# Values and sums of two chunks in one slot, two buffers of exponentials, and two small LayerNorm steps on ScalarE

## The chip, the cores and the metric

The kernel runs on one core of one Trainium2 chip. The metric is the device time of the whole program in microseconds, as the median of several executions. Times inside an execution come from one execution recorded by the hardware profiler.

## What is computed

A cross-attention layer with LayerNorm in fp32: x has 16 batches of 512 rows of 512, the context 16 batches of 77 rows of 512; there are 16 heads of 32.

```
Q = x Wq + bq;  K = ctx Wk + bk;  V = ctx Wv + bv        (16 heads of 32)
attn = softmax(Q K^T / sqrt(32)) over the 77 context rows
out  = (attn V) Wo + bo
result = (out + x - mean) * rsqrt(var + 1e-5) * gamma + beta
```

## The kernel before

The big projections run as three matmuls in TensorE's faster fp32r format: each operand is split into a high part (a ScalarE copy or activation) and a low part (the difference, on GpSimd or VectorE), and high x high, high x low and low x high are summed (xh and xl, qh and ql, ch and cl). `project_context` makes K and part of V first; `attend` does the rest and takes most of the time.

`attend` is a software pipeline of 64 *chunks* g. A chunk is one batch's group of four heads (128 of the 512 columns), so four chunks make a batch, and as many tiles of 128 output rows follow from it. Every engine runs its own `slot(g)` function once per g, in the order written there, through `run`: two rounds of 8 slots and the last ones are written out, the rest is a hardware loop of 8 slots. A slot works on several chunks at different stages; `g.back(n)` is the chunk n slots earlier. Slot g does:

- TensorE: `project_q(g)` into the one bank p_q; `values` and `sums` of chunk g-4 (p_v holds the four heads' values, p_den the sums of the exponentials, from `part` and the selection matrix `sel`); `scores` of g-3 into p_s (two banks, four matmuls a chunk: two after the sums, one each after the second and third step of the output projection); `project_out` of tile g-8 into the one bank p_o, in four steps kc = 0 to 3, one for each chunk of its batch; after each step `rowmax_scores` of g into p_a (two banks, four tiles a chunk).
- ScalarE: `q_high(g)`, the four `exp` of g-3 into `prob`, with `square` of tile g-9 after the second; `load_residual`; `ctx_high` of g-4 (cx to ch), `normalize` of tile g-10, `split_x_high` of x tile g+5 (xt to xh), then the load of a further x tile.
- VectorE: `sum_keys` of g-4 (prob to part), `minus_mean_over_std` of tile g-10 (nmr), `add_residual` of tile g-9 (frees p_o), `q_low`, `invert_sums` (rec, then its transposed spread rden) and `divide` (p_v by rden into cx) of g-4, `variance_of_squares` of g-9 (ve), four `row_maxima` of g, and `turn_maxima` in odd slots.
- GpSimd: `scale` and `shift` of tile g-11, `add_bo` of g-8, `ctx_low` of g-4 (cx - ch to cl), `inverse_std` of g-9 (rstd), `split_x_low` of x tile g+5 (xt - xh to xl).
- SyncE issues the loads of K, V, the q splits rearranged by head (z) and the row maxima, and the stores of finished tiles after `shift`.

There is one `prob`, one `part`, one `rec`, one p_v bank. `project_out` of a batch's first tile (t = 0) waits at kc = 0 for ch and cl of all four chunks (lines 647 to 649):

```
if t == 0:
    pe.wait_ge(ch_ready, m.over(QT, 1, KC))
    pe.wait_ge(cl_ready, m.over(QT, 1, KC))
```

`m.over(QT, 1, KC)` counts the chunks up to the end of tile m's batch. The first tile of batch b is projected in slot 4b + 8; the batch's last chunk, 4b + 3, has its values in slot 4b + 7. Two of the p banks serve at the end for other things (gamma_tail and beta_tail, the last tiles' p_o).

Of the kernel before, what the change touches and what calls it, by code (L numbers as in the profile page):

```python
# [26 lines left out]
P = 128  # L27
D = 512
# [75 lines left out]
def project_context(nc, a, keep, kh_dram, kl_dram, v_dram, B, S2):  # L104
# [12 lines left out]
    with ExitStack() as ctx:  # L117
# [33 lines left out]
        with nc.Block() as block:  # L151
# [172 lines left out]
def attend(nc, a, keep, kh_dram, kl_dram, v_dram, out, B, S, S2):  # L324
# [21 lines left out]
    with ExitStack() as ctx:  # L346
# [6 lines left out]
        def sem(name):  # L353
# [20 lines left out]
        ysum, ssd, nmean = (sb(n, [P, 4, 1], F32) for n in ("ysum", "ssd", "nmean"))  # L374
        p_q, p_v, p_den, p_o = (psum(n) for n in ("p_q", "p_v", "p_den", "p_o"))
# [25 lines left out]
        mv_ready, ve_ready, nmr_ready, const_dve, y_last_scaled, y_last_done, nmean_ready, rows_tail = (  # L401
            sem(n) for n in ("mv_ready", "ve_ready", "nmr_ready", "const_dve", "y_last_scaled", "y_last_done", "nmean_ready", "rows_tail"))
# [12 lines left out]
        gamma_tail, beta_tail = p_s[1], p_den  # L415
# [160 lines left out]
        def _(pe):  # L576
# [14 lines left out]
            def rowmax_scores(g, t):  # L591
# [27 lines left out]
            def values(g):  # L619
# [4 lines left out]
                at_least(pe, cx_ready, g.over(1))  # L624
                for j in range(HC):
                    h = HC * (g.k % NCH) + j
                    nc.tensor.matmul(p_v[DK * j:DK * (j + 1), :], vb[0:S2, g.k // NCH % 2, DK * h:DK * (h + 1)],  # L627
                                     prob[0:S2, j, :], start=True, stop=True)

            def sums(g):  # L630
# [3 lines left out]
                for j in range(HC):  # L634
                    last = nc.tensor.matmul(p_den[DK * j:DK * (j + 1), 0:QB], sel[:], part[:, QB * j:QB * (j + 1)],  # L635
# [44 lines left out]
            def slot(g):  # L680
# [6 lines left out]
                if v.valid(NG) and g.valid(NG):  # L687
                    values(v)
                    sums(v)
# [3 lines left out]
                if not g.valid(NG):  # L693
                    values(v)
# [18 lines left out]
        def _(act):  # L713
            def exp(g, j):
                act.wait_ge(s_summed, g.over(1, 0, HC) + j + 1)
                if j == 0:
                    if g.is_first():
                        act.wait_ge(const_pool, 2)
                    at_least(act, pv_summed, g.over(1))
                    at_least(act, part_ready, g.over(1))  # L720
                nc.scalar.activation(prob[0:S2, j, :], p_s[j % 2][0:S2, :], ACT.Exp, scale=SCALE).then_inc(prob_ready, 1)  # L721
# [26 lines left out]
            def square(m):  # L748
# [4 lines left out]
                                     accum_out=ssd[:, i, :]).then_inc(squared, 1)  # L753

# [113 lines left out]
        def _(dve):  # L868
# [15 lines left out]
            def sum_keys(g):  # L884

                dve.wait_ge(prob_ready, g.over(1, 1, HC))
                at_least(dve, pv_summed, g.over(1))
                nc.vector.tensor_reduce(part[:], prob[0:KP, :, :].rearrange("p h (i r) -> p (h i) r", r=DK),  # L888
                                        AX_X, ALU.add, apply_transpose=True).then_inc(part_ready, 1)

            def invert_sums(g):

                dve.wait_ge(pv_summed, g.over(1, 1))
                at_least(dve, rden_ready, g.over(1))
                nc.vector.reciprocal(rec[:], p_den[:, 0:QB]).then_inc(rec_ready, 1)
                dve.wait_ge(rec_ready, g.over(1, 1))
                at_least(dve, cx_ready, g.over(1))
                nc.vector.transpose(rden[:].rearrange("p (i r) -> p i r", r=DK),  # L898
                                    rec[:].unsqueeze(2).broadcast_to([P, QB, DK])).then_inc(rden_ready, 1)
# [13 lines left out]
            def divide(g):  # L913
# [4 lines left out]
                nc.vector.tensor_tensor(cx[:, i, :], p_v[:], rden[:], ALU.mult).then_inc(cx_ready, 1)  # L918
# [33 lines left out]
            def slot(g):  # L952
# [3 lines left out]
                if v.valid(NG):  # L956
                    sum_keys(v)
                if g.back(LAG_NORMALIZE).valid(NS):
# [5 lines left out]
                if v.valid(NG):  # L964
                    invert_sums(v)
                    divide(v)
                if m.valid(NS):
# [45 lines left out]
            invert_sums(Slot(0, NG - 1))  # L1013
            divide(Slot(0, NG - 1))
# [24 lines left out]
        def _(pool):  # L1039
# [4 lines left out]
            nc.gpsimd.memset(prob[DK * 2:KP, :, :], 0.0).then_inc(const_pool, 1)  # L1044
# [148 lines left out]
```

## Time and profile before

| | us |
|---|---|
| median of 3 runs (lowest to highest) | 623.35 (622.33 to 623.76) |
| profiled execution, its own time | 622.21 |
| its span, first to last instruction | 620.4 |
| TensorE matmuls busy | 594.8 (96%) |
| VectorE busy | 496.9 (80%) |
| ScalarE busy | 362.9 (58%) |
| GpSimd busy | 443.7 (72%) |

The profile's records name an instruction by its line, its engine, its operation, and out<-in by the names of the tiles. PE is TensorE, PEld its weight loads, DVE VectorE, ACT ScalarE, POOL GpSimd. A matmul's record is longer than the step to the next one, because matmuls overlap; the difference of two starts is what one costs. The fp32 matmuls of values and sums appear as two records each.

### The profile page before, as it was taken

How to read it: one execution, taken by the hardware profiler on the slowest of the kernel's cores; microseconds unless marked ns; L12 is line 12 of the kernel's file. 1: busy time of each engine (PE TensorE's matmuls, PEld its weight loads, DVE VectorE, ACT ScalarE, POOL GpSimd, SP SyncE). 2: the span in 40 equal slices, each digit the busy share in tenths (PEclk: the TensorE clock that was granted, in tenths of full speed). 3: DMA queues.
4: the chain of work that ended last, by engine and by line, in shares of the span. 5: the costliest groups of instructions: out<-in, count | busy, mean ns of one | idle time of the engine just before them, and what ended most of it. 6: DMA issues, size and time to landing. Idle time of an engine off the chain costs nothing.

```text
span 620.4 us, 12034 instructions
## 1 busy us (share of the span) xinstructions
PE 594.8 (96%) x3336; PEld 430.5 (69%) x3336; DVE 496.9 (80%) x913; ACT 362.9 (58%) x674; POOL 443.7 (72%) x395
## 2 busy tenths in 40 slices
PE   5998999999999999999999999999999999999992
PEld 5986765677777777777777777777777777777562
DVE  5423468888888888888888888888888888898776
ACT  5621235566666666666666666666666666655562
POOL 1335024648888888888888888888888888888785
PEclk9999999999999999999999999999999999999997
DMA  8859878988979898989898987979897989796523
GB/s 306 308 224 185 205 181 224 206 189 193 235 192 232 212 215 214 224 203 219 201 229 205 221 226 193 235 201 227 207 219 205 211 218 231 196 221 168 168 76 128
DMA packets 93392, 129.58 MB, mean 209 GB/s; under 512 B 49936, under 2 KB 49936, under 8 KB 93360
## 3 DMA queue, kind: packets, MB, share of 16 engines
q1 hardware_dynamic: 74352, 94.42, 60.8%
q10 hardware_dynamic: 19008, 34.78, 21.8%
q8 instruction: 15, 0.25, 0.2%
q14 instruction: 17, 0.14, 0.1%
HBM read 53.94 MB, written 24.35 MB: 126 GB/s over the span
## 4 chain that ended last, share of the span: by engine, by line
PE 87%; DVE 3%; issue 1%; ACT 1%; DVEq 0%; ACTq 0%
PE p_q L586 29%; PE p_o L652 27%; PE p_s L616 10%; PE p_v L627 10%; PE p_a L602 6%; PE p_o L99 3%; DVE nm L933 1%; PE p_a L669 1%; PE p_den L635 1%; DVE rden L898 0%; PE p_q L669 0%; ACT prob L721 0%; DVE part L888 0%; PE p_s L669 0%; ACT qh L736 0%
## 5 line engine op out<-in xcount | busy, mean ns | idle before, releaser
L721 ACT ACTIVATE prob<-p_s 77x512 f32<-77x512 f32 x256 | 143.2, 591 | 103.3 <-PE p_s L616 93.0
L1069 POOL TENSOR_TENSOR cl<-cxt,ch 128x512 fp32r<-128x512 f32 x64 | 83.1, 1299 | 110.0 <-ACT ch L746 110.0
L933 DVE TENSOR_REDUCE nm<-p_a 128x4 f32<-128x308 f32 x256 | 115.9, 475 | 49.1 <-PE p_a L602 48.0
L888 DVE TRANSPOSE_TENSOR_REDUCE part<-prob 96x64 f32<-96x2048 f32 x64 | 146.4, 2287 | 1.6 <-issue 1.3
L736 ACT ACTIVATE qh<-p_q,bq_col 128x512 fp32r<-128x512 f32 x64 | 44.0, 687 | 124.6 <-PE p_q L586 124.6
L586 PE MATMUL p_q<-xh,wqh 128*128 128x512 f32 x256 | 101.1, 395 | 1.7 <-PEq L151 1.7
L586 PE MATMUL p_q<-xl,wqh 128*128 128x512 f32 x256 | 101.2, 395 | 0.0
L586 PE MATMUL p_q<-xh,wql 128*128 128x512 f32 x256 | 101.0, 394 | 0.0
L616 PE MATMUL p_s<-z,ks 97*77 97x512 f32 x256 | 95.6, 413 | 2.4 <-ACT prob L721 2.4
L652 PE MATMUL p_o<-woh,ch 128*128 128x512 f32 x240 | 95.4, 398 | 0.8 <-issue 0.7
L652 PE MATMUL p_o<-wol,ch 128*128 128x512 f32 x240 | 94.6, 394 | 0.0
L652 PE MATMUL p_o<-woh,cl 128*128 128x512 f32 x240 | 94.3, 393 | 0.0
L1050 POOL TENSOR_TENSOR xl<-xt,xh 128x512 fp32r<-128x512 f32 x60 | 77.2, 1287 | 20.0 <-ACT xh L728 20.0
L602 PE MATMUL p_a<-kb,qh 128*128 128x308 f32 x256 | 79.0, 311 | 2.9 <-DVE nm L933 2.8
L1064 POOL TENSOR_TENSOR y<-y,beta_row 128x512 f32<-128x512 f32 x58 | 75.3, 1299 | 4.5
L1076 POOL TENSOR_TENSOR xn<-xn,bo_row 128x512 f32<-128x512 f32 x60 | 77.5, 1291 | 0.0
L1060 POOL TENSOR_TENSOR y<-y,gamma_row 128x512 f32<-128x512 f32 x58 | 74.5, 1285 | 0.0
L627 PE MATMUL p_v<-prob,vb 77*32 77x512 f32 x512 | 68.2, 605 | 0.0
L602 PEld LDWEIGHTS p_a<-kb,qh 128*128 128x128 f32 x256 | 48.3, 189 | 22.9 <-DVE nm L933 7.7
L925 DVE SCALAR_TENSOR_TENSOR ql<-p_q,bq_col,qh 128x512 fp32r<-128x512 f32 x64 | 47.9, 748 | 17.0 <-ACT qh L736 13.5
L652 PEld LDWEIGHTS p_o<-woh,ch 128*128 128x128 f32 x240 | 45.3, 189 | 17.3 <-issue 3.8
L586 PEld LDWEIGHTS p_q<-xh,wqh 128*128 128x128 f32 x256 | 48.0, 188 | 13.3 <-issue 2.1
(128 smaller groups left out, 930.1 us busy)
## 6 DMA issues: line engine op xcount, KB each, us to landing
z<-qh SPq DMA_DIRECT2D x256, 128.0 KB, 3.8
z<-ql SPq DMA_DIRECT2D x124, 128.0 KB, 4.8
xn<-in_x ACTq DMA_DIRECT2D x60, 256.0 KB, 3.3
out_dram<-y SPq DMA_DIRECT2D x60, 256.0 KB, 4.3
xt<-in_x_t ACTq DMA_DIRECT2D x58, 256.0 KB, 5.0
ks<-k_high SPq DMA_DIRECT2D x32, 154.0 KB, 4.8
cx<-in_ctx_t SPq DMA_DIRECT2D x4, 616.0 KB, 6.0
k_high<-kth SPq DMA_DIRECT2D x4, 616.0 KB, 3.6
```

What stands on the lines that cost most here:

```text
L586: last = nc.tensor.matmul(p_q[:], w[:, kc, P * c:P * (c + 1)], x[:, i, kc, :], start=(kc == 0 and n == 0), stop=(kc == KC - 1 and n == 2))
L602: nc.tensor.matmul(p_a[t % 2][:, 0:HC * S2], qh[:, g.k // 2 % 2, g.k % 2, P * t:P * (t + 1)], kb[g.k // NCH % 2][:, g.k % NCH, :], start=T ...
L616: nc.tensor.matmul(p_s[j % 2][0:S2, :], ks[0:KR, g.k // NCH % 2, h, :], z[0:KR, i, j, g.k % 2, :], start=True, stop=True).then_inc(s_summe ...
L627: nc.tensor.matmul(p_v[DK * j:DK * (j + 1), :], vb[0:S2, g.k // NCH % 2, DK * h:DK * (h + 1)], prob[0:S2, j, :], start=True, stop=True)
L652: last = nc.tensor.matmul(p_o[:], x[:, i, kc, P * t:P * (t + 1)], w[:, kc, :], start=(kc == 0 and n == 0), stop=(kc == KC - 1 and n == 2))
L721: nc.scalar.activation(prob[0:S2, j, :], p_s[j % 2][0:S2, :], ACT.Exp, scale=SCALE).then_inc(prob_ready, 1)
L888: nc.vector.tensor_reduce(part[:], prob[0:KP, :, :].rearrange("p h (i r) -> p (h i) r", r=DK), AX_X, ALU.add, apply_transpose=True).then_i ...
L933: nc.vector.tensor_reduce(nm[:, t, g.k % 2:HALF:2], p_a[t % 2][:, 0:HC * S2].rearrange("p (h k) -> p h k", k=S2), AX_X, ALU.max, negate=Tr ...
L1050: nc.gpsimd.tensor_tensor(xl[:, i, n.k % KC, :], xt[:, n.k % 2, :], xh[:, i, n.k % KC, :].bitcast(F32), ALU.subtract).then_inc(xl_ready, 1)
L1064: nc.gpsimd.tensor_tensor(rows(m), rows(m), beta[:], ALU.add).then_inc(y_done, 1)
L1069: nc.gpsimd.tensor_tensor(cl[:, i, g.k % NCH, :], cx[:, g.k % 2, :], ch[:, i, g.k % NCH, :].bitcast(F32), ALU.subtract).then_inc(cl_ready, 1)
L1076: nc.gpsimd.tensor_tensor(xn[:, m.k % 2, :], xn[:, m.k % 2, :], bo[:], ALU.add).then_inc(xb_ready, 1)
```

## The change

TensorE's `values` and `sums` of two chunks now come together in odd slots (`values_of_pair`): p_v has two banks, and one set of four matmuls sums both chunks into 32 columns of p_a's first bank, behind the 308 that the row maxima use. The odd slot's first `rowmax_scores` therefore waits for the reciprocal of those sums, which is one for both chunks; the sums wait for the maxima that read that bank. `prob`, `part` and `rec` have two buffers. The last four chunks (`single`) go one by one as before, with p_v[1] for their sums.

With w = g-5, the chunk before g-4: VectorE does `spread` (the transposition, now by itself) and `divide` of the even chunk in the odd slot (w there) and of the odd chunk at the start of the next even slot (w there); its `sum_keys` of the even chunk stands after the second row maximum of the even slot. ScalarE's `ctx_high` follows: at the end of an odd slot for the even chunk, first in the even slot for the odd one. GpSimd does both `ctx_low` in the even slot: of e = g-6 first, and of w after `scale` and `shift`. `project_out` waits for ch and cl of one chunk at each kc instead of all four at kc = 0.

In slots of the loop the variance moves from VectorE to ScalarE (`variance`, after `square`), and so does the mean over the deviation (`mean_over_std`, two operations, ahead of `normalize`); in the tail VectorE does them as before. The scratch memory for GpSimd-issued DMAs is set to 2048.

```diff
+        den_pair = p_a[0][:, HC * S2:HC * S2 + 2 * QB]
+        den_single = p_v[1][:, 0:QB]
...
 def rowmax_scores(g, t):
+                if t == 0 and g.k % 2 == 1 and g.back(LAG_PV).valid(NG):
+                    pe.wait_ge(rec_ready, g.back(LAG_PV).over(1, 1))
...
+            def values_of_pair(g):
+                at_least(pe, cx_ready, g.over(1, -1))
+                values(g.back(1))
+                values(g)
+                pe.wait_ge(part_ready, g.over(1, 1))
+                at_least(pe, rec_ready, g.over(1, -1))
+                at_least(pe, max_ready, g.over(1, LAG_PV, QT) - 1)
+                for j in range(HC):
+                    last = nc.tensor.matmul(den_pair[DK * j:DK * (j + 1), :].rearrange("p (i r) -> p i r", r=QB), sel[:],
+                                            part[:, :, QB * j:QB * (j + 1)], start=True, stop=True)
+                last.then_inc(pv_summed, 2)
...
 def project_out(m, kc):
-                    if t == 0:
-                        pe.wait_ge(ch_ready, m.over(QT, 1, KC))
-                        pe.wait_ge(cl_ready, m.over(QT, 1, KC))
                     at_least(pe, y_ready, m.over(1))
+                if t == 0:
+                    pe.wait_ge(ch_ready, m.over(QT, 0, KC) + kc + 1)
+                    pe.wait_ge(cl_ready, m.over(QT, 0, KC) + kc + 1)
...
 # TensorE's slot
-                if v.valid(NG) and g.valid(NG):
-                    values(v)
-                    sums(v)
+                if v.valid(NG) and g.valid(NG) and g.k % 2 == 1:
+                    values_of_pair(v)
...
 def exp(g, j):
-                    at_least(act, pv_summed, g.over(1))
-                    at_least(act, part_ready, g.over(1))
+                    at_least(act, pv_summed, pair_end(g.back(2)))
+                    at_least(act, part_ready, g.over(1, -1))
...
+            def variance(m):
+                i = m.k % 4
+                act.wait_ge(squared, m.over(1, 1))
+                nc.scalar.activation(ve[:, i, :], ssd[:, i, :], ACT.Identity, bias=keep["eps"][:],
+                                     scale=1.0 / D ** 3).then_inc(ve_ready, 1)
+            def mean_over_std(m):
+                i = m.k % 4
+                act.wait_ge(rstd_ready, m.over(1, 1))
+                nc.scalar.mul(over_d[:, i, :], rstd[:, i, :], -1.0 / D).then_inc(over_d_ready, 1)
+                act.wait_ge(over_d_ready, m.over(1, 1))
+                nc.scalar.activation(nmr[:, i, :], ysum[:, i, :], ACT.Copy, scale=over_d[:, i, :]).then_inc(nmr_ready, 1)
...
 # ScalarE's slot
+                w = v.back(1)
+                if g.k % 2 == 0 and w.valid(NG) and not single(w):
+                    ctx_high(w)
                 if g.valid(NG):
                     q_high(g)
...
                     square(m)
+                    if g.valid(NG):
+                        variance(m)
...
                     exp(s, 3)
-                if v.valid(NG):
+                if g.k % 2 == 1 and w.valid(NG) and not single(w):
+                    ctx_high(w)
+                if v.valid(NG) and single(v):
                     ctx_high(v)
+                if g.back(LAG_NORMALIZE).valid(NS) and g.valid(NG):
+                    mean_over_std(g.back(LAG_NORMALIZE))
...
 # VectorE's slot
+                w = v.back(1)
+                if g.k % 2 == 0 and w.valid(NG) and not single(w):
+                    spread(w)
+                    divide(w)
-                if v.valid(NG):
+                if v.valid(NG) and (g.k % 2 == 1 or not g.valid(NG)):
                     sum_keys(v)
...
+                if v.valid(NG) and not single(v) and g.k % 2 == 1:
+                    invert_sums(v)
+                    spread(w)
+                    divide(w)
...
                         row_maxima(g, t)
+                        if t == 1 and v.valid(NG) and g.k % 2 == 0:
+                            sum_keys(v)
...
 # GpSimd's slot
+                w, e = v.back(1), v.back(2)
+                if g.k % 2 == 0 and e.valid(NG) and not single(e):
+                    ctx_low(e)
                 if g.back(LAG_SCALE).valid(NS):
                     scale(g.back(LAG_SCALE))
                     shift(g.back(LAG_SCALE))
+                if g.k % 2 == 0 and w.valid(NG) and not single(w):
+                    ctx_low(w)
                 if b.valid(NS):
                     add_bo(b)
-                if v.valid(NG):
+                if v.valid(NG) and single(v):
                     ctx_low(v)
```

## Rows read from the trace of the kernel before

**Rows 1.** The page's chain that ended last, by line, shares of the span.
```profile
PE p_q L586 29%; PE p_o L652 27%; PE p_s L616 10%; PE p_v L627 10%; PE p_a L602 6%; PE p_o L99 3%; DVE nm L933 1%; PE p_a L669 1%; PE p_den L635 1%; DVE rden L898 0%; PE p_q L669 0%; ACT prob L721 0%; DVE part L888 0%; PE p_s L669 0%; ACT qh L736 0%
```

**Rows 2.** Busy us (instructions) in 295 to 345 us: PE, PEld, DVE, ACT, POOL, clock, DMA.
```profile
295.00:345.00 50.00, 50.00 (x291) 35.98 (x290) 43.85 (x83) 32.38 (x62) 41.36 (x37) 1.00 0.87 211
```

**Rows 3.** Timeline of TensorE, slot 31: start us, length us, engine, line, operation.
```profile
302.30 0.39 PE L586 MATMUL p_q<-xh,wqh 128*128 128x512 f32 x1
...
304.85 0.39 PE L586 MATMUL p_q<-xh,wql 128*128 128x512 f32 x1
305.18 1.06 PE L627 MATMUL p_v<-prob,vb 77*32 77x512 f32 x8
306.06 0.23 PE L635 MATMUL p_den<-part,sel 96*32 96x16 f32 x8
306.22 0.69 PE L616 MATMUL p_s<-z,ks 97*77 97x512 f32 x2
...
309.38 0.39 PE L616 MATMUL p_s<-z,ks 97*77 97x512 f32 x1
...
309.75 0.40 PE L652 MATMUL p_o<-woh,ch 128*128 128x512 f32 x1
...
310.45 0.30 PE L602 MATMUL p_a<-kb,qh 128*128 128x308 f32 x1
310.59 0.39 PE L586 MATMUL p_q<-xh,wqh 128*128 128x512 f32 x1
```

**Rows 4.** Wait list: who waited for whom: us in total, times, longest us.
```profile
POOL cl L1069 <- ACT ch L746: 110.0, 62, 8.0
```

**Rows 5.** Timeline of ScalarE, border of slots 31 and 32; idle time before in brackets.
```profile
309.14 1.25 ACT L721 ACTIVATE prob<-p_s 77x512 f32<-77x512 f32 x2 [0.65 <-PE p_s L616]
...
310.30 0.61 ACT L746 CAST ch<-cxt 128x512 fp32r<-128x512 f32 x1
...
311.52 0.62 ACT L728 CAST xh<-xt 128x512 fp32r<-128x512 f32 x1
```

**Rows 6.** Timeline of GpSimd, from the border of slots 31 and 32.
```profile
310.99 1.30 POOL L1069 TENSOR_TENSOR cl<-cxt,ch 128x512 fp32r<-128x512 f32 x1 [1.35 <-ACT ch L746]
...
312.76 1.29 POOL L1050 TENSOR_TENSOR xl<-xt,xh 128x512 fp32r<-128x512 f32 x1
314.00 1.29 POOL L1060 TENSOR_TENSOR y<-y,gamma_row 128x512 f32<-128x512 f32 x1
315.38 1.30 POOL L1064 TENSOR_TENSOR y<-y,beta_row 128x512 f32<-128x512 f32 x1
316.63 1.30 POOL L1076 TENSOR_TENSOR xn<-xn,bo_row 128x512 f32<-128x512 f32 x1
```

**Rows 7.** Timeline of VectorE, slots 31 and 32.
```profile
306.95 0.71 DVE L898 STREAM_TRANSPOSE rden<-rec 128x512 f32<-128x512 f32 x1
...
310.79 0.48 DVE L933 TENSOR_REDUCE nm<-p_a 128x4 f32<-128x308 f32 x1 [0.36 <-PE p_a L602]
311.30 0.31 DVE L950 STREAM_TRANSPOSE nmt<-nm 128x128 f32<-128x128 f32 x1
311.93 2.31 DVE L888 TRANSPOSE_TENSOR_REDUCE part<-prob 96x64 f32<-96x2048 f32 x1 [0.32 <-issue]
...
314.25 0.68 DVE L880 SCALAR_TENSOR_TENSOR y<-p_o,xn 128x512 f32<-128x512 f32 x1
...
314.86 0.74 DVE L925 SCALAR_TENSOR_TENSOR ql<-p_q,bq_col,qh 128x512 fp32r<-128x512 f32 x1
315.52 0.24 DVE L895 RECIPROCAL rec<-p_den 128x16 f32<-128x16 f32 x1
```

**Rows 8.** Groups by line and shape: busy us, mean ns of one | idle us before, releasers.
```profile
L910 DVE TENSOR_SCALAR nmr<-ysum,rstd 128x1 f32<-128x1 f32 x59 | 10.0, 169 | 0.1
...
L210 ACT ACTIVATE kth<-pk,bk_col 128x360 fp32r<-128x360 f32 x8 | 4.3, 561 | 2.2 <-PE pk L301 2.2
...
L210 ACT ACTIVATE kth<-pk,bk_col 128x512 fp32r<-128x512 f32 x4 | 2.8, 688 | 7.4 <-PE pk L301 5.1 <-DMA k_low<-ktl 2.3
```

More of the change, by code:

```diff
@@ L373, in attend @@
         ve, rstd, nmr = (sb(n, [P, 4, 1], F32) for n in ("ve", "rstd", "nmr"))
-        ysum, ssd, nmean = (sb(n, [P, 4, 1], F32) for n in ("ysum", "ssd", "nmean"))
-        p_q, p_v, p_den, p_o = (psum(n) for n in ("p_q", "p_v", "p_den", "p_o"))
+        ysum, ssd, nmean, over_d = (sb(n, [P, 4, 1], F32) for n in ("ysum", "ssd", "nmean", "over_d"))
+        p_q, p_o = (psum(n) for n in ("p_q", "p_o"))
+        p_v = [psum(f"p_v{i}") for i in range(2)]
         p_s = [psum(f"p_s{i}") for i in range(2)]
@@ L412, in attend @@
                       (p_s[0], prob_ready, NG * HC)]
-        gamma_tail, beta_tail = p_s[1], p_den
+        gamma_tail, beta_tail = p_s[1], p_v[1]
         x_last = [xt[:, 0, :], xt[:, 1, :], bv_row[:], vb[:, B % 2, :]]
@@ L434, in last_tile, with single, pair_end @@
             return None
+        den_pair = p_a[0][:, HC * S2:HC * S2 + 2 * QB]
+        den_single = p_v[1][:, 0:QB]
+        def single(v):
+            return isinstance(v.u, int) and PAIR * v.u + v.k >= NG - LAG_PV
+        def pair_end(v):
+            return v.over(1, 1) if single(v) else Slot(v.u, v.k | 1).over(1, 1)
         def is_last(c):
@@ L623, in values @@
                     pe.wait_ge(vb_in[g.k // NCH % 2], g.over(PAIR, 1, 16))
-                at_least(pe, cx_ready, g.over(1))
+                bank = p_v[0] if single(g) else p_v[g.k % 2]
                 for j in range(HC):
                     h = HC * (g.k % NCH) + j
-                    nc.tensor.matmul(p_v[DK * j:DK * (j + 1), :], vb[0:S2, g.k // NCH % 2, DK * h:DK * (h + 1)],
-                                     prob[0:S2, j, :], start=True, stop=True)
+                    nc.tensor.matmul(bank[DK * j:DK * (j + 1), :], vb[0:S2, g.k // NCH % 2, DK * h:DK * (h + 1)],
+                                     prob[0:S2, g.k % 2, j, :], start=True, stop=True)
+            def values_of_pair(g):
[9 more added lines that the diff above has]
+                last.then_inc(pv_summed, 2)
             def sums(g):
@@ L634, in sums @@
                 for j in range(HC):
-                    last = nc.tensor.matmul(p_den[DK * j:DK * (j + 1), 0:QB], sel[:], part[:, QB * j:QB * (j + 1)],
+                    last = nc.tensor.matmul(den_single[DK * j:DK * (j + 1), :], sel[:], part[:, g.k % 2, QB * j:QB * (j + 1)],
                                             start=True, stop=True)
@@ L893, in invert_sums, with spread @@
                 dve.wait_ge(pv_summed, g.over(1, 1))
[L894 to L896 removed]
+                at_least(dve, rden_ready, g.over(1, 0 if single(g) else -1))
+                if single(g):
+                    nc.vector.reciprocal(rec[:, g.k % 2, :], den_single).then_inc(rec_ready, 1)
+                else:
+                    nc.vector.reciprocal(rec[:], den_pair.rearrange("p (i r) -> p i r", r=QB)).then_inc(rec_ready, 2)
+            def spread(g):
+                dve.wait_ge(rec_ready, pair_end(g))
                 at_least(dve, cx_ready, g.over(1))
                 nc.vector.transpose(rden[:].rearrange("p (i r) -> p i r", r=DK),
[L899 removed]
+                                    rec[:, g.k % 2, :].unsqueeze(2).broadcast_to([P, QB, DK])).then_inc(rden_ready, 1)
             def variance_of_squares(m):
                 i = m.k % 4
+                if PAIR * m.u + m.k == NG - LAG_NORM:
+                    dve.wait_ge(rstd_ready, NG - LAG_NORM)
                 dve.wait_ge(squared, m.over(1, 1))
@@ L955, in slot @@
                     add_residual(m)
-                if v.valid(NG):
+                w = v.back(1)
[3 more added lines that the diff above has]
+                if v.valid(NG) and (g.k % 2 == 1 or not g.valid(NG)):
                     sum_keys(v)
-                if g.back(LAG_NORMALIZE).valid(NS):
+                if g.back(LAG_NORMALIZE).valid(NS) and not g.valid(NG):
                     minus_mean_over_std(g.back(LAG_NORMALIZE))
@@ L1013, in _ @@
             invert_sums(Slot(0, NG - 1))
+            spread(Slot(0, NG - 1))
             divide(Slot(0, NG - 1))
```

36 lines of the change are left out of this document (21 added, 15 removed).

## The prediction

> **What bounds the kernel now.** I read the page's chain of waits first: over 80% of it are TensorE's lines, the projections p_q (29%) and p_o (27%), then p_s and p_v at 10% each [rows 1]. The busy times by stretch say the same of the middle: TensorE busy for all of 50 us at a granted clock of 1.00 [rows 2]. So while the pipeline is full, one slot's time is the time of its matmuls, and whatever shortens TensorE's list shortens the kernel, as long as nothing new makes it wait. I therefore read the timelines of TensorE, ScalarE, GpSimd and VectorE around the border between slot 31 (from 302.30) and slot 32 (from 310.59) [rows 3, 5 to 7], since 32 is a slot in which a new batch's output projection begins (k a multiple of 4). The other engines have spare time: the wait list shows GpSimd waiting 110 us for ch over 62 waits [rows 4], some 1.7 us a slot. Spare time is an average, though; what the change has to pass is the order inside one slot.
>
> **TensorE's own list.** In slot 31 the last p_q starts at 304.85 and the first p_s at 306.22, 1.37 us later, where neighbouring matmuls of 512 columns are 0.23 apart (eleven steps from 302.30 to 304.85) [rows 3]. In an even slot the values and sums go away: minus 1.37 - 0.23 = 1.14 us. The odd slot gets a second set of values: p_v at 305.18 to p_den at 306.06 is 0.88 us a set [rows 3]; its weights load while the set before streams. The joint sums have 32 columns for 16. The old step from p_den to p_s is 0.16 us, so the extra is between nothing and another 0.16; I take 0.01, since 16 more columns are little beside 512. A pair of slots gets 1.14 - 0.88 - 0.01 = 0.25 us shorter, bounds 0.10 (sums twice as long) and 0.32 (the p_s pair, which runs 0.06 behind its step after the sums, recovers too). There are 28 pairs in slots 8 to 63: minus 7.0 us, bounds 2.8 and 9.0.
>
> **VectorE.** Half of the reciprocals, the variance and the mean leave it in the loop (0.24 us for a reciprocal [rows 7], 0.17 for the mean [rows 8]); it is not on the chain, so this earns nothing by itself. What matters is that spread and divide of the odd chunk now open the even slot, ahead of add_residual, and that the values no longer stand between p_q and p_o there. Counted from the last p_a of an odd slot (310.45): the maximum starts at 310.79 and its turn at 311.30 [rows 7]; spread would start at about 311.6 and take 0.71, divide start at 312.35, add_residual at 313.0 and be ready 0.69 later, at 313.7, 3.2 after p_a (these operations follow each other in some 0.61 to 0.66, as y, ql and rec do from 314.25 to 315.52 [rows 7]). TensorE needs p_o's bank after 0.14 + 12 x 0.23 + 2 x 0.23, 3.4. The copy to ch and q_high behind divide give qh after 3.85, against a first p_a at 4.1. Both pass with 0.2 us to spare: cost nothing, bound 0.3 a pair. In the odd slot, p_a's first bank now waits for the joint reciprocal. Counted from the start of the even slot, 7.1 us long: its second p_a at 5.05, 0.34 later the maximum (0.4), then sum_keys 2.3, two maxima 0.8, sum_keys 2.3, add_residual 0.61, ql 0.66 and rec 0.24, together 12.7, or 5.6 us into the odd slot; TensorE gets to its p_a there after 6.05 (12 p_q, 1.8 of values, 0.2 of sums, two p_s, three p_o). Behind p_a on TensorE stands the whole rest of the slot, so each of these margins would be paid in full if missed.
>
> **The new order on ScalarE and GpSimd, and the wait it makes.** Chunk 4b+3 is the last of its batch. Its spread and divide now happen in slot 4b+8, the slot in which project_out of that batch's first tile begins. The change lets project_out wait for the chunks one at a time, so only its fourth step (kc = 3) needs cl of 4b+3. But on GpSimd this ctx_low is fourth in its slot, behind ctx_low of 4b+2, scale and shift, and the last thing of GpSimd's slot before is split_x_low, which waits for ScalarE's split_x_high, in turn the last thing of ScalarE's slot, behind the fourth exp. That exp waits for the fourth p_s, late in TensorE's slot. So the chain runs from TensorE to TensorE:
> - p_s of slot 31 starts at 309.38 [rows 3]; the second exp of the 1.25 us pair starts at 309.80, ch at 310.30, xh at 311.52 and it ends at 312.14 [rows 5].
> - New ahead of xh are two one-column ScalarE operations, each waiting for the one before on its own engine. No such operation stands in the trace: the same activation takes 561 ns on 360 columns and 688 on 512 [rows 8], a straight line that leaves about 0.26 us for none. Two of them with some 0.05 for each wait: 0.6 us. Lower bound 0.3 (VectorE's price for two small ones), upper 0.95. xh ends at 312.74.
> - GpSimd then does the split 1.24 (312.76 to 314.00), ctx_low 1.25, scale 1.38 (314.00 to 315.38), shift 1.25 (315.38 to 316.63) and ctx_low of 4b+3, 1.30 in full [rows 6]: 6.42 us, so cl is there at about 319.25. The chunk itself is no obstacle: its ch would be ready some 3.1 us into the slot, at 313.7.
> - TensorE gets to kc = 3 at 309.75 - 302.30 = 7.45 us into an old slot [rows 3], and 1.14 earlier in an even one: 310.59 + 6.31 = 316.90.
>
> TensorE stands still for 2.35 us with everything else of the slot queued behind it. It can't be won back: from there to the next fourth p_s of an odd slot three slots later TensorE has no slack, and the chain starts anew from that p_s. In slots with k = 2 mod 4 the same cl comes as late, but nothing asks for it yet. The wait needs a split in the slot before (the last is in slot 58) and a scale and shift in its own (from slot 11 on): slots 12, 16, ... 56, so 12 times. 12 x 2.35 = plus 28.2 us; bounds 12 x 1.9 and 12 x 2.9 (the two small operations, and 0.2 for GpSimd's rows, which are rough).
>
> The Trainium skill ("ScalarE: Activation LUTs", Rules for kernel authors) gives simple multiplies and adds to VectorE, not ScalarE. The rows agree: the mean is one operation of 0.17 us there [rows 8] and two of about 0.26 here. By that rule, with the mean left on VectorE, the wait would be 0.6 shorter and the sum below 7 us lower, still a loss.
>
> **The rest.** Variance sits on ScalarE between square and the third exp; that exp waited for p_s in slot 31 (0.65 us idle in its row, the DMA issue included [rows 5]), and by these spacings it still starts no later than the fourth p_s allows: nothing, bound 0.2 a slot. SP's store waits for shift, now some 7.4 us into the even slot; behind it stand the z loads of the next slot, which wait for ql, some 5 us into that slot, so it costs nothing. No DMA is added and GpSimd issues none, so the smaller scratch costs nothing. The second buffer of exponentials frees exp from the sums of the chunk before, which only the tail can use. Before slot 8 the stages are filling and TensorE is not full; two pairs there and fewer VectorE operations: minus 1.5, bounds 0 and 3. After slot 63, spread and divide of chunk 59 (1.4 us) come ahead of sum_keys, partly repaid by the freed exp: plus 0.5, bounds -1 and +1.5.
>
> **Sum.** The profiled execution took 622.2 us (span 620.4). 622.2 - 7.0 + 28.2 - 1.5 + 0.5 = 642.4. That execution lies 1.1 under the median of 623.35, so on the median's footing 643.5.
>
> **Rivals.**
> - *The wait is hidden (faster).* If GpSimd reaches ctx_low of 4b+3 before 6.3 us of the slot, only TensorE's shorter list is left: 622.2 - 7.0 - 1.5 + 0.5 = 614.2, or 615.3 on the median. For it: GpSimd is idle 1.7 us a slot on average [rows 4], and the waits per chunk were split just here. Against it: the idle time lies ahead of the split, waiting for xh, so it can't be used. It decides at 2.35 us of error in a chain whose members are all rows but 0.6 us. A half-sized wait (1.2 us) would give 628.6, or 629.7; the gain is eaten up from 0.67 us of wait on (8.0 / 12).
> - *Further waits in every pair (slower still).* If the 0.2 us margins at p_o's bank, qh or the reciprocal are missed by 0.3, 28 x 0.3 = 8.4: 652. For it: three margins under half a microsecond with nothing behind them. Against: the stalled slot gives VectorE 2.35 us every fourth slot.
> - *The change does nothing at all* (TensorE reloads and drains between the two value sets for about 0.25, and the wait is hidden): 623.
>
> **How the numbers follow.** The wait as computed 0.77, further waits 0.11, hidden or nearly so 0.10, nothing 0.02. Measured times of this kernel tell differences of 0.2% (1.2 us) from none, so slower is 0.77 + 0.11 = 0.88, same 0.02, faster 0.10. The computed case reaches from 635 to 651 with its bounds; taking in the half-sized wait and part of the further waits I give 630 to 655, and leave 615 outside.
>
> **What would show it.** In the profile after: TensorE's weight load for p_o waiting for GpSimd's cl, about 12 times and some 2.4 us each, 28 us in the wait list; GpSimd's xl waiting for ScalarE's xh in odd slots; even slots of about 7.1 us and 9.5 us in turn, odd ones of 9.15; nm, rec and y hardly waited for by TensorE. A wait list without cl under p_o proves the main step wrong and leaves the rival of 615; waits of p_o for y or p_a for rec and qh show the second rival. If xh ends less than 0.3 or over 0.95 later than before against its p_s, only the size of the wait was wrong.

## The result: 656.9 us, 5.4% slower, and the profile after

The changed kernel takes 656.86 us (median of 5, 656.57 to 660.08) beside 623.6 of the kernel before in the same rounds: a ratio of 1.0543, 95% interval 1.0526 to 1.0561. The forecast was 643.5, within 630 to 655: the direction held, the size did not. The profiled execution is the longest of the five, 660.08 (span 658.0, mean granted clock 0.970); the other four have 656.6 to 657.0 at about 0.975.

The wait that the prediction computed is there. The page's chain of waits by engine, before and then after, now has GpSimd first, where TensorE stood:

```profile
PE 87%; DVE 3%; issue 1%; ACT 1%; DVEq 0%; ACTq 0%
...
POOL 40%; PE 25%; issue 21%; DVE 4%; ACT 1%; POOLq 0%; DVEq 0%; ACTq 0%
```

The wait list after (total us, times, longest) names the place: p_o's matmul waits for cl exactly 12 times. Its weight load waits there too, put down to "issue" (12 of that row's 17 times). The waits that would have shown the second rival are small:

```profile
POOL xl L1125 <- ACT xh L756: 114.5, 34, 10.4
...
PEld p_o L680 <- issue: 34.0, 17, 2.6
...
PE p_o L680 <- POOL cl L1144: 25.1, 12, 2.3
...
PEld p_o L680 <- DVE y L933: 2.4, 11, 0.8
PE p_a L617 <- DVE nm L996: 2.2, 5, 0.5
```

TensorE at the border of slots 31 and 32, to lay beside [rows 3] (start, length, engine, line, operation, idle time before):

```profile
316.08 0.40 PE L599 MATMUL p_q<-xh,wqh 128*128 128x512 f32 x1
...
324.02 0.39 PE L631 MATMUL p_s<-z,ks 97*77 97x512 f32 x1
...
325.24 0.39 PE L599 MATMUL p_q<-xh,wqh 128*128 128x512 f32 x1
...
329.01 0.47 PE L680 MATMUL p_o<-woh,ch 128*128 128x512 f32 x1 [0.34 <-ACT ch L774]
...
333.98 0.47 PE L680 MATMUL p_o<-woh,ch 128*128 128x512 f32 x1 [1.75 <-POOL cl L1144]
```

The row at 329.01 is kc = 0. It names ch, but kc = 0 asks only for the ch of its batch's first chunk, which is long done; y, which it also waits for, ends 0.25 us before it:

```profile
328.08 0.68 DVE L933 SCALAR_TENSOR_TENSOR y<-p_o,xn 128x512 f32<-128x512 f32 x1
```

ScalarE there, beside [rows 5], with the two new operations of the mean:

```profile
324.95 0.61 ACT L774 CAST ch<-cxt 128x512 fp32r<-128x512 f32 x1
325.46 0.20 ACT L794 ACTIVATE over_d<-rstd 128x1 f32<-128x1 f32 x1
325.69 0.29 ACT L796 ACTIVATE nmr<-ysum,over_d 128x1 f32<-128x1 f32 x1
326.02 0.82 ACT L823 ACTIVATE y<-y,nmr,rstd 128x512 f32<-128x512 f32 x1
326.37 0.36 ACTq L809 DMA_DIRECT2D xt<-in_x_t  x1
326.74 0.60 ACT L756 CAST xh<-xt 128x512 fp32r<-128x512 f32 x1
```

And GpSimd, beside [rows 6]:

```profile
327.42 1.30 POOL L1125 TENSOR_TENSOR xl<-xt,xh 128x512 fp32r<-128x512 f32 x1 [2.42 <-ACT xh L756]
328.67 1.30 POOL L1144 TENSOR_TENSOR cl<-cxt,ch 128x512 fp32r<-128x512 f32 x1
329.92 1.31 POOL L1135 TENSOR_TENSOR y<-y,gamma_row 128x512 f32<-128x512 f32 x1
331.32 1.28 POOL L1139 TENSOR_TENSOR y<-y,beta_row 128x512 f32<-128x512 f32 x1
332.56 1.28 POOL L1144 TENSOR_TENSOR cl<-cxt,ch 128x512 fp32r<-128x512 f32 x1
```

From the start of p_s (324.02) to the end of xh (327.34) are 3.32 us, forecast 3.36; the five GpSimd operations take 6.42, as forecast. kc = 3 starts 333.98 - 325.24 = 8.74 into the slot (8.70 to 8.75 in all twelve; forecast 8.66). In slot 60, which has no split before it, it starts at 6.24 (forecast 6.31). The wait, the difference of the two, is 2.49 us on average where 2.35 stood. A pair of slots without it takes 7.09 + 9.16 = 16.25 instead of 16.55: -0.30, forecast -0.25.

What the sum did not have is in the granted clock (the sixth figure behind the comma, counts in brackets left out). First the stretches around slot 20's wait, then the wait of slot 32 with slot 33; before, [rows 2] had 1.00:

```profile
213.40:223.30 9.90, 9.90 (x46) 7.52 (x44) 7.39 (x15) 8.80 (x20) 7.33 (x8) 1.00 0.88 224
223.30:225.70 2.40, 0.12 (x2) 0.10 (x1) 2.08 (x2) 2.33 (x6) 2.40 (x3) 1.00 0.85 192
225.70:226.24 0.54, 0.54 (x3) 0.44 (x4) 0.00 (x0) 0.12 (x1) 0.54 (x1) 1.00 1.30 176
226.24:229.65 3.41, 3.41 (x10) 2.74 (x9) 2.60 (x2) 0.00 (x0) 3.41 (x4) 0.50 1.02 251
229.65:233.50 3.85, 3.85 (x33) 1.95 (x33) 1.80 (x6) 0.79 (x2) 2.60 (x3) 1.00 0.17 38
...
331.50:334.00 2.50, 0.75 (x5) 0.35 (x3) 2.50 (x3) 2.22 (x6) 2.50 (x3) 1.00 0.44 143
334.00:344.06 10.06, 10.06 (x61) 7.03 (x61) 7.39 (x12) 4.62 (x11) 7.19 (x7) 1.00 0.86 198
```

In slot 20 TensorE stands still for 2.29 us, starts again at 225.63, and 0.6 us later is granted 0.50 (1.2 GHz) for 3.41 us. Its matmuls of 512 columns, 0.23 apart before, are then 0.43 apart (227.23, 227.66, 228.09). This happens behind 7 of the 12 waits (slots 12, 20, 28, 36, 44, 52, 56; idle 2.26 to 2.32 us), and the odd slot behind them takes 10.43 to 10.71 us instead of 9.16. In the other five (16, 24, 32, 40, 48) part of the lost time already lies at kc = 0 (0.34 in the rows of slot 32), the idle time at kc = 3 is shorter, 1.73 to 1.76 us and 2.03 in slot 16, and the clock stays at 1.00 (the last two lines).

The Trainium skill ("TensorE: Matmul & The Clock Gate", HAM oscillation) describes a kernel whose repeated waits, of some 3 to 5 us, each end in a stretch at half clock. Of the shorter waits here, the rows of slots 20 and 21 agree with that, those of slots 32 and 33 do not.

The spans, 658.0 against 620.4, split by the starts of slots (first p_q of each):

| stretch | before | after | difference | forecast |
|---|---|---|---|---|
| up to slot 0 | 47.8 | 48.8 | +1.0 | 0 |
| slots 0 to 8 | 72.3 | 71.0 | -1.2 | -2.6 (-1.5, and -1.14 for the even slot 8) |
| slots 9 to 62 | 447.4 | 480.4 | +33.0 | +21.5 |
| slot 63 and behind | 52.9 | 57.8 | +4.9 | +1.4 (+0.5, and +0.89 for the odd slot 63) |

The third line is 27 pairs x -0.30 = -8.1, twelve stalled slots of 9.65 instead of 7.09 = +30.7, and what the slots with lowered clock take beyond these 9.65 and 9.16: +10.7. Together 33.3.

### The profile page after: what moved, and what is told of

Same layout as the page of the kernel before. It is cut to its first block, busy times and chain, and to the rows that moved or that the text cites. A ratio compares the mean times of both kernels' runs of the same rounds, so it can differ in the third digit from the quotient of the medians.

```text
span 658.0 us, 11546 instructions
## 1 busy us (share of the span) xinstructions
PE 604.0 (92%) x3096; PEld 436.8 (66%) x3096; DVE 478.7 (73%) x774; ACT 401.9 (61%) x837; POOL 445.3 (68%) x396
## 3 DMA queue, kind: packets, MB, share of 16 engines
q1 hardware_dynamic: 74352, 94.42, 57.3%
## 4 chain that ended last, share of the span: by engine, by line
POOL 40%; PE 25%; issue 21%; DVE 4%; ACT 1%; POOLq 0%; DVEq 0%; ACTq 0%
POOL cl L1144 9%; POOL y L1135 9%; PE p_q L599 8%; POOL xl L1125 7%; PE p_o L680 6%; POOL xn L1151 6%; POOL y L1139 5%; POOL rstd L1131 3%; PE p_v L642 3%; PE p_o L99 3%; PE p_s L631 2%; PE p_a L617 2%; DVE nm L996 1%; DVE part L941 1%; ACT prob L749 1%
## 5 line engine op out<-in xcount | busy, mean ns | idle before, releaser
L749 ACT ACTIVATE prob<-p_s 77x512 f32<-77x512 f32 x256 | 141.0, 589 | 85.9 <-PE p_s L631 70.7
L996 DVE TENSOR_REDUCE nm<-p_a 128x4 f32<-128x308 f32 x256 | 118.1, 470 | 71.8 <-PE p_a L617 69.9
L680 PE MATMUL p_o<-woh,ch 128*128 128x512 f32 x240 | 98.1, 409 | 27.7 <-POOL cl L1144 25.1
L599 PE MATMUL p_q<-xh,wqh 128*128 128x512 f32 x256 | 105.4, 412 | 1.7 <-PEq L151 1.7
L599 PE MATMUL p_q<-xl,wqh 128*128 128x512 f32 x256 | 104.4, 408 | 0.0
L599 PE MATMUL p_q<-xh,wql 128*128 128x512 f32 x256 | 104.3, 408 | 0.0
L680 PE MATMUL p_o<-woh,cl 128*128 128x512 f32 x240 | 96.4, 402 | 0.0
L631 PE MATMUL p_s<-z,ks 97*77 97x512 f32 x256 | 93.5, 406 | 1.2 <-ACT prob L749 1.0
L988 DVE SCALAR_TENSOR_TENSOR ql<-p_q,bq_col,qh 128x512 fp32r<-128x512 f32 x64 | 47.8, 747 | 48.9 <-ACT qh L764 48.9
L642 PE MATMUL p_v<-prob,vb 77*32 77x512 f32 x512 | 62.9, 606 | 2.4 <-DVE cxt L981 2.4
L1131 POOL TENSOR_TENSOR rstd<-ve,minus_half 128x1 f32<-128x1 f32 x64 | 35.3, 551 | 43.6 <-ACT ve L787 41.1
## 6 DMA issues: line engine op xcount, KB each, us to landing
cx<-in_ctx_t SPq DMA_DIRECT2D x4, 616.0 KB, 5.6
k_high<-kth SPq DMA_DIRECT2D x4, 616.0 KB, 3.4
```

Of the source, the lines that this page charges most:

```text
L599: last = nc.tensor.matmul(p_q[:], w[:, kc, P * c:P * (c + 1)], x[:, i, kc, :], start=(kc == 0 and n == 0), stop=(kc == KC - 1 and n == 2))
L631: nc.tensor.matmul(p_s[j % 2][0:S2, :], ks[0:KR, g.k // NCH % 2, h, :], z[0:KR, i, j, g.k % 2, :], start=True, stop=True).then_inc(s_summe ...
L680: last = nc.tensor.matmul(p_o[:], x[:, i, kc, P * t:P * (t + 1)], w[:, kc, :], start=(kc == 0 and n == 0), stop=(kc == KC - 1 and n == 2))
L749: nc.scalar.activation(prob[0:S2, g.k % 2, j, :], p_s[j % 2][0:S2, :], ACT.Exp, scale=SCALE).then_inc(prob_ready, 1)
L996: nc.vector.tensor_reduce(nm[:, t, g.k % 2:HALF:2], p_a[t % 2][:, 0:HC * S2].rearrange("p (h k) -> p h k", k=S2), AX_X, ALU.max, negate=Tr ...
```

## The experiments

Theory: the chain of the prediction makes the wait, and the wait costs more than its length because the clock falls behind it. Rivals: the clock or the time depends on something else that the change does (the statistics on ScalarE, the joint sums); the tail has its own cause.

| run | median us (n) | ratio to before, 95% | slots 9 to 62 | tail | stretches at 0.50 in slots 9 to 62 |
|---|---|---|---|---|---|
| the change | 656.86 (5) | 1.0543 [1.0526, 1.0561] | 480.4 | 57.8 | 7 |
| e1 | 619.56 (4) | 0.9939 [0.9922, 0.9955] | 441.6 | 56.5 | 0 |
| e2 | 642.96 (4) | 1.0321 [1.0304, 1.0339] | 465.1 | 56.4 | 1 |
| e3 | 626.88 (4) | 1.0054 [1.0036, 1.0073] | 448.6 | 56.4 | 0 |
| e4 | 624.0 (10) | 1.0015 [1.0005, 1.0025] | 447.4 | 53.7 | 0 |
| e5 | 716.49 (4) | 1.1493 [1.1466, 1.1519] | 532.7 | 59.0 | 12 |
| e6 | 621.93 (10) | 0.9979 [0.9968, 0.9991] | 441.5 | 57.3 | 0 |
| e7 | 620.84 (10) | 0.9959 [0.9931, 0.9987] | 440.5 | 59.4 | 0 |
| e8 | 617.35 (4) | 0.9906 [0.9882, 0.9931] | 440.6 | 55.2 | 0 |
| e9 | 654.26 (4) | 1.0496 [1.0477, 1.0515] | 472.7 | 57.0 | 0 |
| e10 | 618.63 (5) | 0.9916 [0.9899, 0.9933] | 441.5 | 57.3 | 0 |
| e11 | 615.98 (4) | 0.9883 [0.9865, 0.9901] | 440.5 | 53.5 | 0 |
| e12 | 619.49 (6) | 0.9932 [0.9909, 0.9956] | 443.2 | 55.8 | 0 |

Slots 9 to 62, the tail (from slot 63's start to the end) and the stretches at 0.50 are read in each run's profiled execution. That execution can lie off the median: e6's is 1.8 us under it, e11's 0.8 under, e7's 1.8 over, e10's and e12's 1.4 over. Tails that differ by less than this are not told apart here; where it matters, the medians decide.

**e1: ctx_low of the last chunk ahead of scale and shift.**

```diff
 # GpSimd's slot
+                if g.k % 2 == 0 and w.valid(NG) and not single(w):
+                    ctx_low(w)
                 if g.back(LAG_SCALE).valid(NS):
                     scale(g.back(LAG_SCALE))
                     shift(g.back(LAG_SCALE))
-                if g.k % 2 == 0 and w.valid(NG) and not single(w):
-                    ctx_low(w)
```

> The changed kernel with one edit: GpSimd's ctx_low of the odd chunk goes ahead of scale and shift in even slots. Theory G (the loss is the chain from the odd slot's fourth p_s through exp, xh, xl, two ctx_low to project_out's fourth step, plus the lowered TensorE clock after its long waits): cl comes 1.38 + 1.25 = 2.63 us earlier, against a wait of 2.48, so the 12 waits go (29.8 us) and with them the halved clock inside the loop (about 11 us): 656.9 - 41 = 616, no p_o wait for cl over 0.3 us; the end of the program stays as long as in the changed kernel. Rival P (the joint values and VectorE's new order cost by themselves, the GpSimd wait only shows it): another wait takes its place, over 640.

The 12 waits for cl are gone from the wait list, the clock doesn't fall in slots 9 to 62, and they take 441.6, 5.8 less than before: with this order on GpSimd undone, the loop's loss is gone. The total is 3.6 us above what I expected: slots 16, 24, 32, 40 and 48 now wait for y at kc = 0 (7.4 to 7.7 instead of 7.09, 2.6 together), and the tail is 3.5 longer than before.

**e2: the mean back on VectorE. e3: the split right behind the fourth exp.** Two ways to shorten the same chain by different amounts.

```diff
 # e2, ScalarE's slot
-                if g.back(LAG_NORMALIZE).valid(NS) and g.valid(NG):
-                    mean_over_std(g.back(LAG_NORMALIZE))
...
 # e2, VectorE's slot
-                if g.back(LAG_NORMALIZE).valid(NS) and not g.valid(NG):
+                if g.back(LAG_NORMALIZE).valid(NS):
 # e3, ScalarE's slot: split_x_high(n), last in the slot, moved to stand behind exp(s, 3)
```

> The changed kernel with the mean over the deviation back on VectorE (one operation) in the loop, variance still on ScalarE. Theory G: xh comes 0.55 us earlier, each of the 12 waits shrinks from 2.48 to 1.9, minus 6.6 us; if the clock falls only after the longest waits (in the changed kernel it fell after 7 waits of 2.5 us and after none of the 5 that were split in two), the halved clock in the loop goes as well: 639. If the clock falls whatever the wait's length: 650. Rival P: 657, and VectorE later by 0.08 us a slot.

> The changed kernel with ScalarE's split_x_high moved ahead of ctx_high, the mean and normalize, directly behind the fourth exp. Theory G: in odd slots xh comes 0.5 + 0.55 + 0.7 = 1.75 us earlier and with it GpSimd's split and both ctx_low: waits of 0.7 us, no halved clock in the loop: 656.9 - 12 x 1.75 - 11.4 = 624.5. If GpSimd is simply too loaded in even slots and xh has no part in it, nothing moves: 657. Rival P: 657.

The wait of e2 is 2.0 us (stalled slots of 9.10), that of e3 0.8 (7.90). The wait list of e2:

```profile
PE p_o L680 <- POOL cl L1140: 17.4, 12, 1.8
```

Behind e2's waits the clock falls once in twelve, behind e3's never. From the change to e2 the loop loses 15.2 us; 12 x (9.65 - 9.10) = 6.6 of it is the wait itself, so over half is the clock (7 stretches against 1). The two ScalarE operations of the mean, 0.49 us of work in each slot, so cost 14 us of median.

**e4: the kernel before with only the variance and the mean on ScalarE.** No joint sums, so ctx_low is not moved.

> The kernel before with one part of the change alone: variance and the mean over the deviation on ScalarE in the loop. Theory G: here ctx_high goes ahead of the mean, so cl is not later, and GpSimd gets to its split no earlier than xh comes: 623.5, within 0.3%. A rival that blames ScalarE's longer list by itself (three operations of 0.2 to 0.3 us a slot for 55 slots): up to 0.75 a slot, 655 to 660.

No change in slots 9 to 62 (447.4). The profiled execution's 1.6 us more lie half ahead of slot 0, where nothing was edited, and half in the tail (0.7). On ScalarE, with its idle time, these operations cost nothing where no chain runs through it.

**e5: the change with the old wait at kc = 0 for all four chunks.**

```diff
-                if t == 0:
-                    pe.wait_ge(ch_ready, m.over(QT, 0, KC) + kc + 1)
-                    pe.wait_ge(cl_ready, m.over(QT, 0, KC) + kc + 1)
+                if t == 0 and kc == 0:
+                    pe.wait_ge(ch_ready, m.over(QT, 1, KC))
+                    pe.wait_ge(cl_ready, m.over(QT, 1, KC))
```

> The changed kernel with one part undone: project_out waits for ch and cl of all four chunks at kc = 0 again, as before the change. Theory G: cl comes at the same 8.73 us of the slot, but TensorE now stands from 3.25 us on instead of 6.24, 3.0 us longer, 12 times: plus 36; and with waits of 5.5 us the clock falls after every one of the 12, not 6 or 7 (some 1.6 us each): plus 8 to 10: 700. If the clock had nothing to do with the wait's length: 693.

The waits per chunk are worth 60 us here, more than expected. The clock falls in every one of the 12 waits (5.2 us idle), 0.5 to 2.2 us before TensorE starts again, and in 9 of them for 6.83 us instead of 3.41: I had taken the short stretch for all. I had also left out slots 8 and 60, which wait too (13.55 us instead of 8.55, 9.60 instead of 7.08).

Slot 60 of e5 also shows that the length of a wait doesn't decide by itself. Its wait has the 2.29 us of slot 20 in the change (first line), and the clock stays at 1.00 behind it:

```profile
225.63 0.47 PE L680 MATMUL p_o<-woh,ch 128*128 128x512 f32 x1 [2.29 <-POOL cl L1144]
```
```profile
637.62 0.47 PE L680 MATMUL p_o<-woh,ch 128*128 128x512 f32 x1 [2.29 <-POOL cl L1144]
```
```profile
637.60:650.00 12.40, 12.38 (x71) 8.94 (x72) 9.92 (x14) 5.86 (x13) 7.72 (x8) 1.00 0.72 160
```

**e9: work in the wait.** The first three steps of project_out are done once more ahead of kc = 3 in each batch's first tile.

```diff
+                if t == 0 and kc == KC - 1:
+                    for again in range(KC - 1):
+                        for n, (x, w) in enumerate(((ch, woh), (ch, wol), (cl, woh))):
+                            nc.tensor.matmul(p_o[:], x[:, i, again, P * t:P * (t + 1)], w[:, again, :],
+                                             start=(again == 0 and n == 0), stop=False)
...
```

> The changed kernel, with the first three steps of project_out done once more (from the start, into the same bank) ahead of kc = 3 in the first tile of each batch: nine matmuls, some 2.04 us of work at full clock, that fill most of the wait of 2.48 us. If TensorE's clock falls because TensorE stands idle there, no 1.2 GHz stretch is left in slots 9 to 63, the stalled slots keep their 9.16 us (0.4 of wait left), the odd slots behind them go from 10.45 to 9.17, and the loop's slots 9 to 62 take about 480.4 - 11.4 = 469; slots 8 and 60, which have no wait there, get 2.0 longer each: together 656.9 - 11.4 + 4 = 649.5, down to 647.5 if slot 8 hides its part. If the clock falls for another reason (by the slot's place, or from the chip's load as a whole), the seven stretches stay and the time is 657 to 661.

This is the direct test. cl comes as late as in the change (kc = 3 at 8.79 us of slot 20), TensorE is idle for 0.26 us, and the clock stays at 1.00. Slots 20 and 21 of e9, and its kc = 3:

```profile
217.66:227.37 9.71, 9.45 (x43) 7.11 (x42) 6.87 (x11) 8.09 (x18) 7.46 (x6) 1.00 0.85 217
227.37:236.53 9.16, 9.16 (x59) 6.27 (x57) 7.14 (x11) 4.14 (x9) 6.27 (x7) 1.00 0.79 187
```
```profile
226.45 0.47 PE L685 MATMUL p_o<-woh,ch 128*128 128x512 f32 x1 [0.26 <-POOL cl L1149]
```

All seven stretches are gone and every odd slot from 9 on takes 9.14 to 9.17. The loop is 7.6 us shorter although slot 60 is 2.1 longer and the stalled slots 1.1 together: 10.8 us, the 10.7 of the account. So it is the standing still behind which the clock falls: filled with work, the same wait has no stretch at 0.50. The median lies 4.8 us above the expectation. Of these, 3.2 come from a mistake of mine: I took the clock's cost from the profiled execution of the change and subtracted it from the median. 0.005 less mean clock over 656 us is 3.3 us, just by how much that execution is longer. By this estimate the clock in the loop costs some 7.5 us on the median rather than 10.7.

**e6, e7, e8: the tail, first attempt.** e6 is e1 with VectorE's spread and divide of chunk 59 in slot 63. e7 adds, in even slots, add_residual before spread and divide, and q_high before ctx_high. e8 adds e2's edit.

```diff
 # e6, VectorE's slot 63, after the second row maximum
+                        if t == 1 and is_last(g):
+                            spread(v)
+                            divide(v)
...
 # e7, VectorE's slot (add_residual stays in its old place in odd slots)
+                if m.valid(NS) and g.valid(NG) and g.k % 2 == 0:
+                    add_residual(m)
```

> As e1_ctx_first, and VectorE does spread and divide of chunk 59 in slot 63 (after its second row maximum) instead of at the start of slot 64. In e1 the end from slot 63 on is 56.5 us long against 52.9 before, TensorE stands 2.6 us for the values of chunk 60, and 3.4 us at half clock follow. Theory G (the end is longer for that wait and the clock after it): minus 2.0 for the wait and 1.7 for the clock: 615.9. A rival that puts the longer end on the order of ScalarE's copies and exps there: 619, no change.

> As e6, and in even slots add_residual goes ahead of spread and divide on VectorE, and q_high ahead of ctx_high on ScalarE. In e1 the slots 16, 24, 32, 40 and 48 (first of a loop round) are 0.3 to 0.6 us longer than the other even ones, TensorE's first p_o waiting for y: those 2.4 us should go: 613.5. If ScalarE's later exps make p_s wait instead: 616 or more.

> As e7, with the mean back on VectorE in the loop. In e7 nothing on TensorE should wait for ScalarE's mean any more, so 0.55 us less of ScalarE a slot earns nothing: 613.5, within 0.2% of e7. If cl is still on the edge in every fourth slot, up to 1.2 us faster.

e6 missed: p_v of chunk 60 starts 9.72 us after slot 63 does instead of 12.18, but the tail is no shorter, and the median is 2.4 us above e1's. The copy of chunk 59 still starts at 13.66, as ScalarE issues four loads of z and one of vb first. e7 missed too: slots 9 to 62 gain 1.0 us over e6, the tail of its profiled execution loses 2, with the clock at 0.50 for 10.24 us. e8 gained 3.5 us over e7 where I expected none within 0.2%; slots 9 to 62 are the same, so it lies in the tail, where e8 has no stretch at 0.50 until its last 7 us. Why the mean's place decides that is not shown.

**e10, e11, e12: the tail, second attempt.** ScalarE's ctx_high of chunk 59 also goes into slot 63, ahead of those issues: onto e1 with e6's edit (e10), onto e8 (e11), and onto e1 with e2's and e6's edits but not e7's order (e12).

```diff
 # ScalarE's slot, behind normalize
                 if is_last(g):
+                    ctx_high(v)
```

> e1_ctx_first with both halves of the last pair's work moved up: VectorE's spread and divide of chunk 59 in slot 63, and ScalarE's ctx_high of 59 in slot 63 too, ahead of the DMA issues that ended its slot there. If the tail's extra length (56.5 against 52.9) is the copy of chunk 59 queued behind those issues, cl of 59 comes some 3 us earlier, p_o's fourth step of slot 64 doesn't wait, and the tail is 53 to 54.5: 616.5 to 617.5. The rival: the issues, which then go out after the copy, bring the scores and exps of the last chunks late, or TensorE's half clock moves to another place in the tail; then 619 to 622.

> e8_mean_too with the same move of ScalarE's ctx_high of chunk 59 into slot 63. Its tail was 55.2 without a half clock; by the theory of the queue it comes to 53 to 54 and the whole to 615.5. By the rival (issues later, scores later) it stays at 617.4 or loses a little.

> e1_ctx_first with the mean over the deviation back on VectorE and both moves of the last pair, without the residual's new order of e7: loop as in e1 (441.6, or 440.6 if the mean on ScalarE was what kept the exps late), tail 53 to 54.5: 615 to 616.5. If e7's order of the residual is needed for e11's time, this one stays 1 us above e11.

e11 came out as expected: its tail is 53.5 in the profiled execution, within 0.6 us of before, and from slot 0 to the last 6 us its clock stays at 1.00. In e8, with a tail of 55.2, the p_o of slot 65 starts 18.89 us after slot 63's start, in e11 17.75. e10 and e12 missed by some 1 and 3 us: with the mean still on ScalarE (e10) p_s of slot 64 starts at 15.39 instead of 14.24 and the clock falls at 16.15; without the residual's order (e12) p_o waits for y where e11 does not, and slots 9 to 62 take 2.7 us longer. The wait list of e12, and of e11:

```profile
PE p_o L680 <- DVE y L932: 3.0, 6, 0.9
```
```profile
PE p_o L680 <- DVE y L932: 0.2, 1, 0.2
```

e11 beats both kernels: 1.2% faster than before (0.9865 to 0.9901). It keeps the joint sums and the variance on ScalarE, and orders the rest anew.

## Why the prediction was wrong

*TensorE's list: right.* -0.30 a pair against -0.25, inside its bounds of 0.10 to 0.32.

*The wait: right in place, count and size.* Twelve times, 2.49 us against 2.35. The two small operations are 198 and 295 ns (the last two groups below, the first is the variance; forecast 0.26 each), and the whole chain from p_s to kc = 3 takes 9.96 us against 9.87.

```profile
L787 ACT ACTIVATE ve<-ssd,eps 128x1 f32<-128x1 f32 x55 | 16.2, 295 | 1.8
L796 ACT ACTIVATE nmr<-ysum,over_d 128x1 f32<-128x1 f32 x54 | 15.9, 295 | 1.7
L794 ACT ACTIVATE over_d<-rstd 128x1 f32<-128x1 f32 x54 | 10.7, 198 | 0.0
```

*The price of the wait: the step that failed.* "12 x 2.35 = plus 28.2 us" counts a wait at its own length. Seven of the twelve were followed by TensorE at 1.2 GHz, another 10.7 us in the profiled execution, an estimated 7.5 on the median, which would have been near 649 without them, inside the range. e9 takes these stretches away by giving TensorE something to do while it waits for the same cl. No rival counted such a stretch either; "further waits" came to a similar time by another mechanism, which the wait list excludes. The trace of before could show a hint only at its end, a clock of 0.50 from 613.8 us on; from slot 0 to there it was 1.00.

*The tail: mis-sized,* +4.9 for +1.4 (0.5, with bounds -1 to +1.5, and 0.89 for slot 63's second set of values). The prediction counted 1.4 us of VectorE's work less a gain; what decided is what waits for it. Values of chunk 60 wait for the divide of 59, and TensorE's clock falls in that wait, 0.46 us before it ends:

```profile
612.41 1.94 PE L642 MATMUL p_v<-prob,vb 77*32 77x512 f32 x8 [2.39 <-DVE cxt L981]
```
```profile
560.00:609.90 49.90, 49.90 (x270) 36.48 (x268) 41.99 (x68) 35.94 (x78) 40.12 (x36) 1.00 0.78 201
609.90:611.95 2.05, 0.11 (x1) 0.00 (x0) 1.98 (x6) 1.05 (x2) 2.05 (x2) 1.00 0.90 217
611.95:618.78 6.83, 6.37 (x25) 3.31 (x26) 3.91 (x6) 2.29 (x5) 4.18 (x4) 0.50 0.77 217
```

The same wait stands in e9, without a fall:

```profile
606.90 1.06 PE L642 MATMUL p_v<-prob,vb 77*32 77x512 f32 x8 [2.39 <-DVE cxt L986]
```
```profile
606.95:643.40 36.45, 33.41 (x179) 21.79 (x179) 25.72 (x53) 20.22 (x42) 28.29 (x27) 1.00 0.32 96
```

And ScalarE's copy of 59, moved into slot 64, lands behind five DMA issues that slot 63 makes on its queue (ScalarE after; ACTq is the issue):

```profile
610.17 0.81 ACT L823 ACTIVATE y<-y,nmr,rstd 128x512 f32<-128x512 f32 x1
610.17 2.78 ACTq L873 DMA_DIRECT2D z<-ql  x4
613.00 0.66 ACTq L818 DMA_DIRECT2D vb<-in_x  x1
613.70 0.62 ACT L774 CAST ch<-cxt 128x512 fp32r<-128x512 f32 x1 [2.72 <-issue]
```

The prediction had costed the queues past which SP's store moved, but not those past which this copy moved. From e8 to e11, which move only the copy, the median falls by 1.4 us (616.83 to 618.11 against 615.19 to 616.46). From e6 to e10, again only the copy, it falls by 3.3 (620.13 to 622.95 against 617.23 to 620.05). The move of spread and divide alone (e6) made the median 2.4 longer than e1's. No single edit mends the tail, and how much of the 4.9 each cause has is not separated.

*Fill and margins: inside their bounds.* Slots 0 to 7 are 0.6 us shorter (forecast 1.5, bounds 0 and 3), slot 8 another 0.6 (forecast 1.14). The margins at qh and the reciprocal held. The one at y, counted as passed with 0.2 us to spare, was missed by 0.2 to 0.4 us in five slots (16, 24, 32, 40, 48; 0.34 in slot 32), where it lay inside the longer wait and cost nothing. Its price shows once that wait is gone: 2.6 us together in e1, and e12's waits for y against e11. Of the +1.0 ahead of slot 0, where nothing was edited, nothing is settled: the same stretch takes 48.1 to 49.1 in the other runs.

*Rivals.* "The wait is hidden" gave 615.3 and a decision at 2.35 us of chain: e1 hides it and lands at 619.6, above by the tail and the waits for y; e11 lands at 616.0.

## What to carry to other kernels

Before an operation is moved to a later slot, follow its queue: here a chunk's last subtraction stood behind two LayerNorm operations that nothing on the chain waited for, and moving it two lines up was worth 37 us. Where the bound engine is TensorE at full clock, price a new wait at its length and, in the upper bound, at the half-clock stretch that may come behind it (here from waits of 2.0 us on, 1.5 us a stretch). Let the engine's last slot and the tail be walked through like the loop: a moved operation there meets issues that the loop does not have.

## What the runs showed of the hardware

Whether TensorE's clock falls at a wait goes with the wait's length, but not by that alone. It fell never at 0.8 us (e3), once in 12 at 2.0 (e2), behind 7 of 12 in the change (idle 2.26 to 2.32 us in these 7, 1.73 to 2.03 in the others), and in 12 of 12 in e5, with 5.2 us of idle time. But an idle time of 2.29 us in e5's slot 60 had no fall, one of 2.39 in the tail had one in the change and none in e9, and e2's one fall came behind 1.76 us. When a wait falls may count as well: the six falls in slots 12 to 52 of the change start 71.68 us apart each time, as long as their eight slots take together. No run separates the two. A stretch of 3.41 us at 1.2 GHz cost 1.5 us on average (10.7 / 7). On ScalarE a one-column activation is 295 ns with its bias or scale from a column beside 198 for the plain multiply, and four issues of z loads hold its queue for 2.78 us, 0.7 each, against 0.36 for the load of an x tile.
